# Four engines' loops written out, SyncE's kept, in a four-layer graph network

## The chip, the cores and the metric

The kernel runs on one core of one Trainium2 chip. A core has five engines, each with its own stream of instructions: TensorE (PE, matrix products; PEld is its weight load), VectorE (DVE), ScalarE (ACT), GpSimd (POOL) and SyncE (SP), which here only starts DMA transfers. They meet through semaphores. The metric is the device time of one execution in microseconds (us).

## The reference, cut to what matters

128 graphs of 64 nodes with 512 features pass four layers, each followed by a residual sum and a layer norm. Two graphs make a tile of 128 rows, so there are 64 tiles.

```python
x = _layernorm(x + _L0_gnn_ref(x, adj, W1, b1, gamma, beta, W2, b2))   # hypergraph convolution, ReLU, norm, convolution
x = _layernorm(x + _L1_gnn_ref(x, adj, w, a))                          # A = exp(leaky(8 tanh((s_i + s_j) / 8))) * adj; A @ x @ w
x = _layernorm(x + _L2_gnn_ref(x, adj, W1, b1, W2, b2, W3, b3))        # three layers adj @ (x @ W) + b
x = _layernorm(x + _L3_gnn_ref(x, nodemask, adj, adj, Wqkv, Wout, b))  # attention with 8 heads, plus adj and exp(-adj)
```

## The kernel before

Two stages stand one behind the other, with a barrier between them. `hypergraph_and_pairwise` computes layers 0 and 1 and writes its result to `x2` in HBM; `convolutions_and_attention` reads it and computes layers 2 and 3. Each stage works through 16 groups of CH = 4 tiles. Products with weights are made of three matmuls (high by high, high by low, low by high part), by `products` (L561 in the first stage, L1109 in the second); products with the 64 by 64 adjacency blocks are short ones (L581, L1140, L1171, L1185).

The order of the work is written out by hand, in a string `ORDER` in each stage. An entry such as `t2.3` is a step and a tile; a plus sign means that the tile belongs to the next group, so one pass through the string finishes a group and begins the next. Every engine goes through the same string and does its own part of each step, in `steps(entries, it, reg)`. The steps with a plus sign alone make up START, which runs first; then comes a loop of 15 turns over the whole string; then END, the steps without the sign. START and END are called with `number`, so their waits are on constants. In the loop `it` is a register, and `counts` and the lines after it (L650, L1125 on TensorE, L1016 on VectorE and so on) turn it into a few registers at the head of each turn, which the waits then use.

TensorE's first step in the loop of the first stage is `y2.2` (L561), behind `t3.0` at the end of the turn. In the second stage the string begins with `ta.0 ta.1 av.0 s.2 s.3 av.1 wo.0` and ends with `s.0+ s.1+ sm.0+ sm.1+ qk.1+`: on TensorE `ta` is L1178, `av` L1185, `s` L1171, and `qk`, `wo`, `v` and the `g` steps are L1109. In `av` TensorE waits for the copies of `ta` by ScalarE (L971) and VectorE (L1076). The loops' own instructions carry the lines L673 and L1195 on TensorE. In the first stage the run `t3.3 t2.0 t2.1` on TensorE is made of short matmuls alone (L621, L581). SyncE has loops of its own, with register values in its waits and in the addresses of its transfers.

Of the kernel before, what the change touches and what calls it, by code (L numbers as in the profile page):

```python
# [44 lines left out]
def hypergraph_and_pairwise(nc, semaphores, x, adj, W1T, b1, gamma, beta, W2T, b2, w, wT, a, x2, slots, later):  # L45
# [3 lines left out]
    iters = tiles // CH  # L49
# [5 lines left out]
    with ExitStack() as ctx:  # L55
# [161 lines left out]
        @block.gpsimd  # L217
        def _(pool):

            pool.memset(ident[:, :], 0.0).then_inc(ident0, 1)  # L220
            pool.wait_ge(ident0, 1)
            pool.affine_select(out=ident[:, :], in_=ident[:, :], compare_op=ALU.not_equal, fill=1.0, base=0,
                               pattern=[[-1, P]], channel_multiplier=1).then_inc(consts_ok, 1)
            pool.memset(ones[:, :], 1.0).then_inc(consts_ok, 1)
            pool.memset(mhalf[:, :], -0.5).then_inc(consts_ok, 1)
            pool.wait_ge(vec_in, 5 * 16)
            pool.tensor_scalar(b2_all[:, :], b2_all[:, :], 0.5, None, ALU.mult).then_inc(b2_half, 1)

            def alone(sem, value):

                pool.wait_ge(consts_ok, 3)
                pool.wait_ge(sem, value)

            def rstd(c, n, mv, ve, eps):

                alone(mv, n[c])
                pool.tensor_scalar(col(c, VE), col(c, MV + 1), eps, None, ALU.add).then_inc(ve, 1)
                pool.wait_ge(ve, n[c])
                return pool.tensor_tensor(col(c, RS), col(c, VE), mhalf[:, :], ALU.pow)

            def cur(c, n, each):

                alone(h_ok, each)
                pool.wait_ge(S_sb, each)
                pool.wait_ge(z2, n[c])
                pool.tensor_copy(CU[:, c, :], NX[:, c, :]).then_inc(cur_ok, 1)

            def u(c, n):

                pool.wait_ge(tx_ps, n[c])  # L250
                pool.wait_ge(bias_ok, n[c])
                pool.tensor_tensor(X[:, c, :], X[:, c, :], ubias[:, c, :], ALU.add).then_inc(u_ok, 1)

            def rs_first(c, n):
                rstd(c, n, mv1, ve1, EPS).then_inc(rs1, 1)

            def rs_second(c, n):
                rstd(c, n, mv2, ve2, EPS / 4).then_inc(rs2, 1)

            def rs_third(c, n):  # L260
                rstd(c, n, mv3, ve3, EPS).then_inc(rs3, 1)

            def steps(entries, it, reg):
                at, each = counts(it, reg), [reg(it + (a + 1)) for a in (0, 1)]
                for step, c, ahead in entries:
                    n = at[ahead]
                    if step == "cur":
                        cur(c, n, each[ahead])
                    if step == "u":
                        u(c, n)  # L270
                    if step == "rs1":
                        rs_first(c, n)
                    if step == "rs2":
                        rs_second(c, n)
                    if step == "rs3":
                        rs_third(c, n)

            steps(START, -1, number)
            with pool.Fori(0, iters - 1) as it:
                steps(ORDER, it, pool.to_reg)  # L280
            steps(END, iters - 1, number)

        @block.scalar
        def _(act):
# [58 lines left out]
            def steps(entries, it, reg):  # L343
                at, each = counts(it, reg), [reg(it + (a + 1)) for a in (0, 1)]
                for step, c, ahead in entries:
                    n = at[ahead]
                    if step == "w":
                        w(c)
                    if step == "S":
                        evacuate_S(each[ahead], None if entries is START else at[ahead - 1][CH - 1])  # L350
                    if step == "txe":
                        txe(c, n)
                    if step == "relu":
                        relu(c, n)
                    if step == "gs":
                        gs(c, n)
                    if step == "t2e":
                        t2e(c, n)
                    if step == "f":
                        f(c, n)  # L360
                    if step == "t3e":
                        t3e(c, n)

            steps(START, -1, number)
            with act.Fori(0, iters - 1) as it:
                steps(ORDER, it, act.to_reg)
            steps(END, iters - 1, number)

        @block.vector
        def _(dve):  # L370
# [171 lines left out]

            dve.sem_inc(z2, CH)
            steps(START, -1, number)
            with dve.Fori(0, iters - 1) as it:
                steps(ORDER, it, dve.to_reg)
            steps(END, iters - 1, number)

        @block.tensor
        def _(pe):  # L550
# [119 lines left out]
                        y3(c, n)  # L670

            steps(START, -1, number)
            with pe.Fori(0, iters - 1) as it:  # L673
                steps(ORDER, it, pe.to_reg)
            steps(END, iters - 1, number)

# [8 lines left out]
def convolutions_and_attention(nc, semaphores, x2, adj, mask_rows, mask_cols, E, AA, QK, slots, b1, b2, b3, Wqkv, bout, out):  # L686
# [4 lines left out]
    iters = tiles // CH  # L691
# [4 lines left out]
    with ExitStack() as ctx:  # L696
# [150 lines left out]
        @block.gpsimd  # L847
        def _(pool):
            pool.memset(ident[:, :], 0.0).then_inc(ident0, 1)
            pool.wait_ge(ident0, 1)  # L850
            pool.affine_select(out=ident[:, :], in_=ident[:, :], compare_op=ALU.not_equal, fill=1.0, base=0,
                               pattern=[[-1, P]], channel_multiplier=1).then_inc(consts_ok, 1)
            pool.memset(mhalf[:, :], -0.5).then_inc(consts_ok, 1)
            pool.memset(ln_ld[:, :], LN_LD).then_inc(consts_ok, 1)

            def alone(sem, value):

                pool.wait_ge(consts_ok, 3)
                pool.wait_ge(sem, value)

            def rstd(c, n, ve):

                alone(ve, n[c])
                return pool.tensor_tensor(col(c, RS), col(c, VE), mhalf[:, :], ALU.pow)  # L864

            def cm(n, loaded):

                alone(masks_in, loaded)
                pool.tensor_copy(mcf[:, :, :], mcol[:, :, :]).then_inc(mc_ok, 1)
                alone(mc_ok, n)  # L870
                pool.wait_ge(row_ok, n)
                pool.tensor_tensor(MM[:, :, :, :], MM[:, :, :, :], mcf[:, :, :].rearrange("p g c -> p c g").unsqueeze(3).to_broadcast([P, CH, 2, C]), ALU.mult)\
                    .then_inc(mm_ok, 1)
                pool.tensor_scalar(BT[:, :, :, :], A[:, :, :, :], LG, None, ALU.mult).then_inc(bt3, 1)
                alone(mm_ok, n)
                alone(exp_adj, n)
                pool.tensor_scalar(BS[:, :, :, :], MM[:, :, :, :], MASKED, -MASKED, ALU.mult, ALU.add).then_inc(bs_ok, 1)
                pool.wait_ge(bt3, n)
                pool.tensor_tensor(Cm[:, :, :, :], Cm[:, :, :, :], BT[:, :, :, :], ALU.add).then_inc(cm2, 1)
                pool.wait_ge(cm2, n)  # L880
                pool.tensor_tensor(Cm[:, :, :, :], Cm[:, :, :, :], MM[:, :, :, :], ALU.mult).then_inc(cm_ok, 1)

            def steps(entries, it, reg):
                at = counts(it, reg)
                each = [reg(it + (a + 1)) for a in (0, 1)]
                loaded = [reg(it * (16 * MASK_LOADS) + 16 * MASK_LOADS * (a + 1)) for a in (0, 1)]
                for step, c, ahead in entries:
                    n = at[ahead]
                    if step == "cm":
                        cm(each[ahead], loaded[ahead])  # L890
                    if step == "rs3":
                        rstd(c, n, ve3).then_inc(rs3, 1)
                    if step == "rs4":
                        rstd(c, n, ve4).then_inc(rs4, 1)

            steps(START, -1, number)
            with pool.Fori(0, iters - 1) as it:
                steps(ORDER, it, pool.to_reg)
            steps(END, iters - 1, number)

        def T(W, c):
# [30 lines left out]
        def _(act):  # L932
# [46 lines left out]
                act.wait_ge(load_in[k], 16)  # L979
                act.copy(qkv_parts[k][0], by_head[k]).then_inc(split_hi, 1)  # L980
            steps(START, -1, number)
            with act.Fori(0, iters - 1) as it:
                steps(ORDER, it, act.to_reg)
            steps(END, iters - 1, number)

        @block.vector
        def _(dve):
# [102 lines left out]
                            .then_inc(x4_ok, 1)  # L1090

            steps(START, -1, number)
            with dve.Fori(0, iters - 1) as it:
                steps(ORDER, it, dve.to_reg)
            steps(END, iters - 1, number)

        @block.tensor
        def _(pe):
# [93 lines left out]

            pe.wait_ge(split_lo, len(pieces) + KD)
            steps(START, -1, number)
            with pe.Fori(0, iters - 1) as it:  # L1195
                steps(ORDER, it, pe.to_reg)
            steps(END, iters - 1, number)

# [43 lines left out]
```

## Time and profile before

| | us |
|---|---|
| median of 3 runs | 2844.67 (2843.2 to 2847.39) |
| profiled execution | 2846.66 |
| its span, first to last instruction | 2844.9 |

Busy in that span: TensorE 2659.1 us, its weight loads 2197.8, VectorE 1820.5, ScalarE 879.0, GpSimd 474.9. The mean granted clock of TensorE is 0.978 of full speed. The first stage reaches to about 1150 us, the second fills the rest.

How to read the rows further down: times are us from the start of the span unless marked ns. "L1109" is line 1109 of the kernel. In a list of waits a row names the instruction that waited, what it waited for, the sum, the number of times and the longest. "issue" stands for time in which the engine waited for nothing that the profile shows. In a timeline a row has start, duration, engine, line, operation and count, and in brackets the idle time before it and its cause. The engine's sequencer, which handles branches, registers and waits, is marked by a q behind the engine's name.

### The profile page before, as it was taken

To read this page: it belongs to the slowest core of one execution; us is meant where nothing else is said; L and a number is where in the kernel's file an instruction comes from. 1 tells how busy PE (TensorE), PEld (TensorE's weight loads), DVE (VectorE), ACT (ScalarE), POOL (GpSimd) and SP (SyncE) were. 2 spreads that over 40 slices of the span, in tenths; PEclk is the share of its full clock that TensorE was granted. 3 is DMA by queue.
4 is the path that set the end of the run, shared out by engine and by line. 5 is a ranking of instruction groups with operands and counts; after the bars stand their busy time and mean duration, and the time that the engine had idled before them with its cause. 6 is when DMAs were issued, how large, how long until landed. Compare 5 with 4: busy or idle time off the path is not lost.

```text
span 2844.9 us, 73879 instructions
## 1 busy us (share of the span) xinstructions
PE 2659.1 (93%) x30296; PEld 2197.8 (77%) x30296; DVE 1820.5 (64%) x3754; ACT 879.0 (31%) x2397; POOL 474.9 (17%) x749
## 2 busy tenths in 40 slices
PE   3999999999999999299999999999999999999998
PEld 2778778777777778287788788788788778878877
DVE  3778887788878887446545655654654655565565
ACT  2222322222222222233332332333333333233233
POOL 0222222222222222010110111011011011101101
PEclk9999999999999999699999999999999999999999
DMA  5111111111111110201101100100110110110010
GB/s 181 28 38 36 35 35 35 38 36 36 38 36 40 42 35 19 97 6 33 37 8 33 38 13 28 36 25 19 33 31 13 33 38 10 29 38 17 26 32 16
DMA packets 130004, 99.41 MB, mean 35 GB/s; under 512 B 89104, under 2 KB 91152, under 8 KB 129808
## 3 DMA queue, kind: packets, MB, share of 16 engines
q1 hardware_dynamic: 129808, 96.30, 11.4%
q8 instruction: 184, 3.01, 0.5%
q14 instruction: 12, 0.10, 0.0%
HBM read 62.68 MB, written 33.55 MB: 34 GB/s over the span
## 4 chain that ended last, share of the span: by engine, by line
PE 52%; DVE 4%; issue 2%; ACT 1%; SPq 1%; DMA 0%; DVEq 0%; POOLq 0%
PE qs L1109 43%; PE qs L1140 4%; PE qs L1171 1%; PE qs L1178 1%; DVE T2l L1004 1%; PE qs L1150 1%; PE qs L1185 1%; ACT T2h L942 1%; DVE sm L1007 0%; DVE Z L1084 0%; DVE E L1069 0%; DVE E L1073 0%; DMA QK<-in_L_Wqkv 0%; DVE sm L1060 0%; DVE E L1058 0%
## 5 line engine op out<-in xcount | busy, mean ns | idle before, releaser
L1109 PE MATMUL qs<-hi,T2h 128*128 128x512 f32 x1024 | 422.0, 412 | 24.5 <-DVE T2l L1004 24.1
L1109 PE MATMUL qs<-hi,T2l 128*128 128x512 f32 x1024 | 406.9, 397 | 0.0
L1109 PE MATMUL qs<-lo,T2h 128*128 128x512 f32 x1024 | 406.5, 397 | 0.0
L1004 DVE TENSOR_TENSOR T2l<-qs,T2h 128x512 fp32r<-128x512 f32 x320 | 212.9, 687 | 183.1 <-ACT T2h L942 110.9
L864 POOL TENSOR_TENSOR sm<-sm,mhalf 128x1 f32<-128x1 f32 x128 | 86.2, 673 | 1370.6 <-DVE sm L1011 1370.6
L1109 PE MATMUL qs<-T2h,WQh 128*128 128x256 f32 x1024 | 291.2, 284 | 0.0
L1109 PE MATMUL qs<-T2h,WQl 128*128 128x256 f32 x1024 | 288.2, 281 | 0.0
L1109 PE MATMUL qs<-T2l,WQh 128*128 128x256 f32 x1024 | 288.1, 281 | 0.0
L1109 PEld LDWEIGHTS qs<-hi,T2h 128*128 128x128 f32 x1024 | 194.6, 190 | 78.5 <-DVE T2l L1004 34.8
L1109 PEld LDWEIGHTS qs<-hi,T2l 128*128 128x128 f32 x1024 | 194.5, 190 | 46.1
L1109 PEld LDWEIGHTS qs<-lo,T2h 128*128 128x128 f32 x1024 | 195.1, 190 | 39.8
L561 PE MATMUL ps<-W2h,Th 128*128 128x512 f32 x512 | 204.3, 399 | 5.1 <-issue 4.5
L561 PE MATMUL ps<-W1h,Th 128*128 128x512 f32 x512 | 206.8, 404 | 0.6 <-DVE Tl L411 0.6
L561 PE MATMUL ps<-W1l,Th 128*128 128x512 f32 x512 | 201.4, 393 | 0.0
L561 PE MATMUL ps<-W1h,Tl 128*128 128x512 f32 x512 | 201.2, 393 | 0.0
L561 PE MATMUL ps<-W2h,Tl 128*128 128x512 f32 x512 | 199.7, 390 | 0.0
L561 PE MATMUL ps<-W2l,Th 128*128 128x512 f32 x512 | 199.5, 390 | 0.0
L946 ACT ACTIVATE H<-H 128x512 f32<-128x512 f32 x128 | 81.2, 634 | 368.5 <-DVE H L1032 368.5
L1109 PEld LDWEIGHTS qs<-T2h,WQh 128*128 128x128 f32 x1024 | 192.7, 188 | 1.1
L1109 PEld LDWEIGHTS qs<-T2l,WQh 128*128 128x128 f32 x1024 | 192.8, 188 | 0.0
L1109 PEld LDWEIGHTS qs<-T2h,WQl 128*128 128x128 f32 x1024 | 192.7, 188 | 0.0
L966 ACT ACTIVATE E<-E,sm 128x64 f32<-128x64 f32 x512 | 172.0, 340 | 32.1 <-DVE sm L1062 31.6
(175 smaller groups left out, 5319.3 us busy)
## 6 DMA issues: line engine op xcount, KB each, us to landing
X<-in_x SPq DMA_DIRECT2D x64, 256.0 KB, 6.5
x<-R SPq DMA_DIRECT2D x64, 256.0 KB, 2.0
X<-x SPq DMA_DIRECT2D x64, 256.0 KB, 2.9
out<-Z SPq DMA_DIRECT2D x64, 256.0 KB, 3.1
AB<-in_adj SPq DMA_DIRECT2D x512, 8.0 KB, 1.6
A<-in_adj SPq DMA_DIRECT2D x128, 32.0 KB, 2.2
An<-in_adj SPq DMA_DIRECT2D x16, 128.0 KB, 2.3
WB<-in_adj SPq DMA_DIRECT2D x32, 64.0 KB, 7.3
```

The source lines that it names most:

```text
L561: mm = pe.matmul(out, lhsT, rhs, start=start and i == 0, stop=i == len(terms) - 1)
L864: return pool.tensor_tensor(col(c, RS), col(c, VE), mhalf[:, :], ALU.pow)
L942: act.copy(by_graph(Th, c), halves(c)).then_inc(th[i], 1)
L946: act.activation(H[:, c, :], H[:, c, :], ACT.Relu).then_inc(g_sb[i], 1)
L966: last = act.activation(EH(c)[:, h, :], EH(c)[:, h, :], ACT.Exp, bias=col(c, NB + h), scale=SCALE, accum_out=col(c, SUM + h))
L1004: return dve.tensor_tensor(lo, ps, hi.bitcast(F32), ALU.subtract)
L1109: mm = pe.matmul(out, lhsT, rhs, start=i == 0, stop=i == len(terms) - 1)
L1140: mm = pe.matmul(half[q, k * C:(k + 1) * C], rows[g, k * P + q.start:k * P + q.stop], AT[g, c, :], start=True, stop=True)
L1150: mm = pe.transpose(psA[c][:, k * P:(k + 1) * P], X[:, c, k * P:(k + 1) * P], ident[:, :])
L1171: mm = pe.matmul(ps[c][y * C:(y + 1) * C, x, (n_ * 2 + g) * C:(n_ * 2 + g + 1) * C], QK[x * C:(x + 1) * C, m, rows_g], QK[x * C:(x + 1) * ...
L1178: mm = pe.transpose(ps[c][:, x, n_ * P:(n_ + 1) * P], E[:, c, x * 2 + n_, :], ident[:, :])
L1185: mm = pe.matmul(ps[c][x * C:(x + 1) * C, g, (2 * n_ + y) * C:(2 * n_ + y + 1) * C], H[rows_g, c, h * DHEAD:(h + 1) * DHEAD], AA[rows_g, c ...
```

## The change

In both stages the loop of 15 turns is replaced by 15 calls of `steps` in a row, with plain numbers for `it`, on TensorE, VectorE, ScalarE and GpSimd. Their register instructions and branches are gone, their waits are on constants, and the order of the steps is the same. SyncE keeps its two loops. The edit is the same in eight places:

```diff
             steps(START, -1, number)
-            with pool.Fori(0, iters - 1) as it:
-                steps(ORDER, it, pool.to_reg)
+            for it in range(iters - 1):
+                steps(ORDER, it, number)
             steps(END, iters - 1, number)
...
-            with act.Fori(0, iters - 1) as it:
-                steps(ORDER, it, act.to_reg)
+            for it in range(iters - 1):
+                steps(ORDER, it, number)
...
-            with dve.Fori(0, iters - 1) as it:
-                steps(ORDER, it, dve.to_reg)
+            for it in range(iters - 1):
+                steps(ORDER, it, number)
...
-            with pe.Fori(0, iters - 1) as it:
-                steps(ORDER, it, pe.to_reg)
+            for it in range(iters - 1):
+                steps(ORDER, it, number)
```

## Rows read from the trace of the kernel before

**Rows 1.** The page's busy times: busy us, share of the span, instructions.
```profile
PE 2659.1 (93%) x30296; PEld 2197.8 (77%) x30296; DVE 1820.5 (64%) x3754; ACT 879.0 (31%) x2397; POOL 474.9 (17%) x749
```

**Rows 2.** Waits of TensorE over the whole span: total us, times, longest.
```profile
PE qs L1178 <- issue: 30.1, 14, 2.4
...
PE ps L561 <- issue: 4.5, 14, 0.4
```

**Rows 3.** The loops' own lines on TensorE (L1195, L673): ns min/median/max, first and last start.
```profile
L1195 PEldq COMPARE_BRANCH  x15: 79/3619/3799, 1375.5 to 2809.3; - x15
...
L673 PEldq COMPARE_BRANCH  x15: 76/208/245, 169.7 to 1116.3; - x15
```

**Rows 4.** The chain that ended last, second loop: start, us, what.
```profile
1267.14 11.61 PE qs L1109 x96
...
1292.48 5.86 PE qs L1109 x24
...
1366.09 11.59 PE qs L1109 x96
...
1396.51 5.86 PE qs L1109 x24
...
2799.86 11.59 PE qs L1109 x96
```

**Rows 5.** Timeline of TensorE, opening of turn 0 of the second loop.
```profile
1278.57 1.04 PE L1178 MATMUL qs<-ident,E 128*128 128x128 f32 x8
1280.08 0.69 PE L1185 MATMUL qs<-AA,H 64*64 64x64 f32 x32 [0.47 <-DVE AA L1076]
...
1281.73 0.68 PE L1185 MATMUL qs<-AA,H 64*64 64x64 f32 x32
```

**Rows 6.** Timeline of TensorE, opening of turn 2 of the second loop.
```profile
1483.69 1.09 PE L1178 MATMUL qs<-ident,E 128*128 128x128 f32 x8 [1.98 <-issue]
...
1486.56 0.27 PE L1185 MATMUL qs<-AA,H 64*64 64x64 f32 x1 [0.93 <-issue]
...
1488.24 0.68 PE L1185 MATMUL qs<-AA,H 64*64 64x64 f32 x32
```

**Rows 7.** Stretches: us, busy (count) of PE, PEld, DVE, ACT, POOL, granted clock, DMA.
```profile
187.40:255.00 67.60, 66.99 (x799) 53.94 (x791) 54.23 (x121) 19.22 (x42) 17.75 (x32) 1.00 0.12 37
1278.60:1377.60 99.00, 96.01 (x1106) 81.29 (x1104) 57.46 (x113) 34.04 (x106) 11.76 (x14) 1.00 0.10 28
...
1378.00:1396.00 18.00, 13.90 (x228) 11.28 (x228) 10.36 (x23) 5.83 (x23) 0.59 (x1) 0.81 0.06 17
```

**Rows 8.** Timeline of TensorE, `av.0` in END of the second stage.
```profile
2812.66 0.69 PE L1185 MATMUL qs<-AA,H 64*64 64x64 f32 x32 [0.33 <-ACT AA L971]
```

**Rows 9.** DMA queues in 200:1100, 118:187, 1278.6:1377.6 and 1481.7:1583.9: packets, MB, share.
```profile
q1 hardware_dynamic: 45840, 32.92, 11.7%
...
q8 instruction: 4, 0.07, 0.4%
...
q8 instruction: 10, 0.16, 0.7%
q14 instruction: 2, 0.02, 0.1%
...
q8 instruction: 11, 0.18, 0.8%
```

**Rows 10.** Timeline of TensorE, first loop: start of `S`, end of the short run.
```profile
118.69 0.28 PE L574 MATMUL ps<-HB,HT 64*64 64x64 f32 x4
...
147.57 0.45 PE L581 MATMUL ps<-CU,R 64*64 64x64 f32 x12 [0.66 <-issue]
...
187.37 0.34 PE L574 MATMUL ps<-HB,HT 64*64 64x64 f32 x6
...
213.28 2.39 PE L581 MATMUL ps<-CU,R 64*64 64x64 f32 x126
...
1066.32 0.39 PE L574 MATMUL ps<-HB,HT 64*64 64x64 f32 x7
```

More of the change, by code:

```diff
@@ L896, in _ @@
             steps(START, -1, number)
-            with pool.Fori(0, iters - 1) as it:
-                steps(ORDER, it, pool.to_reg)
+            for it in range(iters - 1):
+                steps(ORDER, it, number)
             steps(END, iters - 1, number)
@@ L981, in _ @@
             steps(START, -1, number)
-            with act.Fori(0, iters - 1) as it:
-                steps(ORDER, it, act.to_reg)
+            for it in range(iters - 1):
+                steps(ORDER, it, number)
             steps(END, iters - 1, number)
@@ L1092, in _ @@
             steps(START, -1, number)
-            with dve.Fori(0, iters - 1) as it:
-                steps(ORDER, it, dve.to_reg)
+            for it in range(iters - 1):
+                steps(ORDER, it, number)
             steps(END, iters - 1, number)
@@ L1194, in _ @@
             steps(START, -1, number)
-            with pe.Fori(0, iters - 1) as it:
-                steps(ORDER, it, pe.to_reg)
+            for it in range(iters - 1):
+                steps(ORDER, it, number)
             steps(END, iters - 1, number)
```

## Prediction, made before the changed kernel was run

> **What bounds the kernel now.** I read four views, in this order. The page's busy times: TensorE is busy 93% of the span [rows 1], so time can only go where TensorE stands still or is fed slowly, and an instruction saved on another engine counts only if TensorE waits for it. Next the waits of TensorE: of the idle time in the loops the largest item isn't a wait for data. It is 30.1 us in 14 pieces ahead of L1178, with "issue" as what ended it, and a second one of 4.5 us in 14 pieces ahead of L561 [rows 2]. A loop of 15 turns jumps back 14 times, L1178 (`ta.0`) is TensorE's first step in the second loop and L561 (`y2.2`) its first in the first loop, so these are the 28 jumps. Then the branch instructions themselves: TensorE's COMPARE_BRANCH lasts 3619 ns (median) in the second loop and 208 ns in the first [rows 3]. The last reading is the length of whole turns, because a jump may cost more than the idle time it is named for.
>
> Call the turns 0 to 14; turn 0 is entered by falling through from START, with no jump, and runs the same 1,104 matmuls on TensorE as every other (1,106 in a stretch that takes in two of its neighbours') [rows 7]. That makes it a specimen of the written-out code inside the old kernel. The last long group of `qk.1` ends at 1267.14 + 11.61 = 1278.75, the next at 1366.09 + 11.59 = 1377.68, the last at 2799.86 + 11.59 = 2811.45 [rows 4]. So turn 0 takes 98.93 us, and turns 1 to 14 take 1433.77 us, 102.41 each: a jump costs 3.48 us, not the 2.15 of the wait's name. The rows show where the rest is. In turn 0 the opening (`ta.0 ta.1 av.0 s.2 s.3 av.1`) is over at 1281.73 + 0.68 = 1282.41, 3.66 us after the turn's start [rows 5]. In turn 2 the first matmul starts after 1.98 us idle, the last matmul of `av.0` waits another 0.93 us with nothing to wait for but its own issue, and the opening ends at 1488.92, 7.2 us after the turn's start at 1481.71 [rows 6]. From the first long group of `g0.0` on, the turns are alike: 1292.48 to 1377.68 is 85.20 us in turn 0, 1396.51 to 1481.71 is 85.20 us in turn 1 [rows 4, 6]. In some turns the granted clock falls after the idle time (0.81 in the 18 us behind the first jump, against 1.00 over all of turn 0 [rows 7]); that is in the 102.41 already and goes with the idle time.
>
> Why the two loops differ is seen in the instruction packets. In the first loop, from 200 to 1100 us, there are none at all: its body stays on the chip. In the second loop a turn brings 11 packets of 16 KB on queue 8, though the code is the same each time, and turn 0 took 10 [rows 9]. Its body doesn't stay, and the jump's target has to be fetched.
>
> **The change, part by part.** *The 14 jumps of the second loop go*, and with them six register instructions at each turn's head. Price: 14 x 3.48 = 48.7 us, all on the path, since TensorE stands still or is starved there. What is late next is known from turn 0: after `ta.1` it is VectorE's copy of `ta` (0.47 us), then the chain through `z4` and `sm.2`, as now.
>
> *The register heads on VectorE.* In turn 0 `av.0` waited 0.47 us for the copy at L1076; in END, which has constants and no head, it waited 0.33 us [rows 5, 8]. The difference of 0.14 us is the nearest row: between 0 and 15 x 0.14 = 2.1 us, taken 1.5. ScalarE's and GpSimd's heads lie in their own idle time: free. Waits on constants instead of registers: the same instructions in the same number, free. SyncE keeps its loops and issues the same DMAs.
>
> *The 14 jumps of the first loop go*: the idle time before L561 is 4.5 us [rows 2], and its turns are otherwise alike, so 4.5.
>
> *What is added is a stream of instructions in the first loop*, where nothing is fetched now. TensorE has some 790 matmuls and as many weight loads a turn [rows 7], about 1,600 instructions. Turn 0 again is the specimen, since its code was fetched (4 packets [rows 9]). It takes 187.37 - 118.69 = 68.68 us, against (1066.32 - 187.37) / 13 = 67.61 for the later ones, and the difference sits in one place: in the run `t3.3 t2.0 t2.1`, 164 short matmuls with no long one between, TensorE stops for 0.66 us by "issue", and the run ends 1.03 us later in its turn (148.02 - 118.69 = 29.33, against 215.67 - 187.37 = 28.30) [rows 10]. So a fetch isn't ahead where a packet's worth of instructions goes by in about 3 us, and only this run is long enough (328 instructions, half of them weight loads). From the packets of the second loop (some 2,250 instructions with the waits, in 9 to 11 packets) a packet holds 205 to 250. It hurts when one packet's instructions lie wholly within the run: (328 - 240) / 240, somewhat over a third of the turns, since the place moves from turn to turn. I take 5 turns of 15 at 1.03; one is paid already, so +4. Bounds: -1 (never) and +14.4 (in every turn).
>
> *The same in the second loop.* Its opening is a run of some 290 instructions (16 + 64 + 128 + 64 and the waits), in which turn 0 met no stop; the other places consist mostly of long matmuls and hide a fetch, as the 10 packets of turn 0 show, behind which the turn is as long as any other. In the opening a stop would be about as dear as in the first loop: bounds 0 and 5 us, taken 1. The other engines have some 40 to 120 busy instructions a turn [rows 7], and waits beside them; turn 0 had two packets of 8 KB on queue 14 [rows 9] and the 85.20 us behind the opening are the same with and without them: free.
>
> **The sum.** -48.7 - 1.5 - 4.5 + 4 + 1 = -49.7 us. The profiled execution took 2846.66 us (span 2844.9 and 1.8 around it); it becomes 2797.0. It lies 2.0 above the median of the runs, 2844.67, so the forecast is 2795.0. With every unknown at its good end: -48.7 - 2.1 - 4.5 - 1 = -56.3, 2788. With every one at its bad end: -48.7 - 4.5 + 14.4 + 5 = -33.8, 2811.
>
> **The rivals.** *Only the named idle time goes* (30.1 + 4.5 = 34.6, result 2810): the slow opening of each turn stays, because its dense code is fetched too late whether a jump stands ahead of it or not. For it speaks that the 0.93 us stop in turn 2 is inside straight code. Against it: turn 0 has the same code fetched in a row and no such stop. 8%.
>
> *Every turn of the first loop pays the 1.03 us*: -48.7 - 1.5 - 4.5 + 14.4 + 1 = -39.3, result 2805. For it: the one specimen paid. Against: the turn's length in instructions is no multiple of a packet's, so the place moves. 8%.
>
> *Slower: the small engines are not fetched ahead.* VectorE has 121 and 113 busy instructions in a turn of the two loops and ScalarE 42 and 106 [rows 7], 382 together; at 100 to 125 in 8 KB (half the count above) that is about 50 places in 15 turns of each loop where a new packet must be there, none of them now. If each cost the 3.6 us of a fetch that nothing anticipates [rows 3], and TensorE waited for all of it, it would be +180, result 2975. It decides from 1.0 us a place. Against it: turn 0 of the second loop has two such packets and no longer tail. 4%.
>
> *The change does nothing on the path* (2845): the 3.6 us of the branch are not its own but a wait put down to it, and come up again at the head of the next turn. Against it, turn 0 once more. 3%.
>
> **How the numbers follow.** The forecast has 77%. The range reaches from the good ends, 2788, to the bad ends, 2811, and so takes in the first two rivals; what is left out is slower, no change, and something more. About 0.2% (6 us) is what a measurement of this kernel can tell from no change. Faster 0.93, same 0.03, slower 0.04.
>
> **What would show it.** No COMPARE_BRANCH on TensorE, no idle time by issue ahead of L1178; periods of 98.8 us in the second loop and 67.3 in the first, with 68.3 in about a third of its turns; stops by issue only at L581, and if in the second loop then at L1185 and L1171; queue 8 up from 184 packets to some 250, with 6 to 8 a turn in the first loop. Wrong would be: VectorE or ScalarE standing still by issue, or periods in the second loop that stay near 102.

## The result, and the profile after

The changed kernel takes 2793.89 us (median of 4 runs, 2793.61 to 2797.75) against 2844.13 for the kernel before: ratio 0.9824, interval 0.9807 to 0.9842, so 50.2 us less. The forecast was 2795.0.

The page of the changed kernel, its busy times, granted clock by 40ths of the span and instruction queues:

```profile
span 2791.6 us, 73091 instructions
...
PE 2634.4 (94%) x30296; PEld 2179.6 (78%) x30296; DVE 1814.2 (65%) x3754; ACT 875.6 (31%) x2397; POOL 474.4 (17%) x749
...
q8 instruction: 240, 3.93, 0.6%
q14 instruction: 70, 0.57, 0.1%
```

The same work in 53.3 us less of span, with 788 instructions fewer (registers and branches). Packets of instructions went from 184 to 240 on queue 8 and from 12 to 70 on queue 14. TensorE's waits (total us, times, longest), to be laid beside [rows 2]:

```profile
PE qs L1109 <- DVE T2l L1004: 29.7, 50, 1.4
PE qs L1178 <- DVE E L1073: 10.1, 17, 0.8
...
PE qs L1185 <- ACT AA L971: 5.3, 16, 0.3
...
PE qs L1140 <- issue: 3.0, 15, 0.2
...
PE ps L581 <- issue: 2.3, 2, 1.2
```

The 30.1 us ahead of L1178 and the 4.5 us ahead of L561 are gone. What is left of idle time by issue is two stops at L581 and the 3.0 us at L1140, which the kernel before has too. Where the time went is read by stretches. The timeline of TensorE after, start of turns 0 and 1 and of END in the second stage (`ta.0`):

```profile
1278.85 0.82 PE L1178 MATMUL qs<-ident,E 128*128 128x128 f32 x6
...
1377.64 0.60 PE L1178 MATMUL qs<-ident,E 128*128 128x128 f32 x4
...
2761.37 0.60 PE L1178 MATMUL qs<-ident,E 128*128 128x128 f32 x4
```

| stretch, us | before | after | difference | forecast |
|---|---|---|---|---|
| start to the second loop's first `ta.0` | 1278.6 | 1278.9 | +0.3 | -0.5 |
| the second loop's 15 turns | 1532.7 | 1482.5 | -50.2 | -49.2 |
| END of the second stage | 33.6 | 30.2 | -3.4 | 0 |
| span | 2844.9 | 2791.6 | -53.3 | -49.7 |

The turns of the second stage now last 98.8 us each (1377.64 - 1278.85 = 98.79; turns 1 to 14 (2761.37 - 1377.64) / 14 = 98.84). The first stage gained nothing. The third line isn't shown to be the change's. Stretches in END (us, busy and count of PE, PEld, DVE, ACT, POOL, granted clock, DMA), first before, then after, then a later kernel with the same second stage (e9 below):

```profile
2811.50:2844.90 33.40, 22.30 (x256) 16.75 (x254) 19.83 (x43) 9.30 (x40) 2.25 (x4) 0.80 0.09 32
```
```profile
2761.50:2791.60 30.10, 18.21 (x257) 13.63 (x255) 19.75 (x43) 9.25 (x40) 2.24 (x4) 0.99 0.10 36
```
```profile
2758.20:2791.40 33.20, 22.09 (x256) 16.85 (x254) 19.84 (x43) 9.26 (x40) 2.24 (x4) 0.80 0.08 32
```

From its first `ta.0`, END lasts 30.2 us in this execution (clock 0.99) and 33.6 in the one before (0.80). e9 has the changed code there and takes 33.4 us at 0.80; e4, whose TensorE runs the code of the kernel before, takes 30.8 at 0.91. So END varies with the clock that an execution is granted, by about as much as the single runs lie apart (2793.6 to 2797.8). This is probably also why the profiled executions differ by 53.1 us and the medians by 50.2; the unprofiled runs don't show their END.

### The profile page after: what moved, and what is told of

The parts are those of the page before. It is cut to its first block, busy times and chain, and to the rows that moved or that the text cites. A ratio compares the mean times of both kernels' runs of the same rounds, so it can differ in the third digit from the quotient of the medians.

```text
span 2791.6 us, 73091 instructions
## 1 busy us (share of the span) xinstructions
PE 2634.4 (94%) x30296; PEld 2179.6 (78%) x30296; DVE 1814.2 (65%) x3754; ACT 875.6 (31%) x2397; POOL 474.4 (17%) x749
## 4 chain that ended last, share of the span: by engine, by line
PE 50%; DVE 5%; ACT 1%; issue 1%; SPq 1%; DMA 0%; DVEq 0%; POOLq 0%; POOL 0%
PE qs L1109 43%; PE qs L1140 4%; DVE T2l L1004 1%; PE qs L1178 1%; PE qs L1150 1%; PE qs L1171 1%; DVE sm L1060 1%; DVE E L1058 1%; ACT T2h L942 1%; PE qs L1185 0%; DVE sm L1007 0%; DVE E L1069 0%; DVE E L1073 0%; DVE Z L1084 0%; DMA QK<-in_L_Wqkv 0%
## 5 line engine op out<-in xcount | busy, mean ns | idle before, releaser
L561 PE MATMUL ps<-W1h,Th 128*128 128x512 f32 x512 | 206.6, 404 | 0.6 <-DVE Tl L411 0.6
L561 PE MATMUL ps<-W2h,Th 128*128 128x512 f32 x512 | 204.5, 399 | 0.6 <-DVE Tl L441 0.6
L561 PE MATMUL ps<-W1l,Th 128*128 128x512 f32 x512 | 201.3, 393 | 0.0
L561 PE MATMUL ps<-W1h,Tl 128*128 128x512 f32 x512 | 201.2, 393 | 0.0
L561 PE MATMUL ps<-W2l,Th 128*128 128x512 f32 x512 | 199.6, 390 | 0.0
L561 PE MATMUL ps<-W2h,Tl 128*128 128x512 f32 x512 | 199.5, 390 | 0.0
```

The lines of the kernel that those rows point to most:

```text
L561: mm = pe.matmul(out, lhsT, rhs, start=start and i == 0, stop=i == len(terms) - 1)
```

## The experiments

**Each stage alone.** In e1 only the second stage is written out, in e2 only the first. The edit is that of the diff above, four places instead of eight.

> Written out on the four engines in the second stage alone; the first stage keeps its loops. My theory (what the change gained is the fetch behind TensorE's jump, which only the second stage pays, and the first stage gained nothing): within 1 us of the changed kernel, 2793 to 2795, ratio to the kernel before 0.982 to 0.983. Rival (each stage gives back its own idle time by issue, 4.5 us of it in the first): 2798.

> Written out on the four engines in the first stage alone. My theory: no change, 2844 to 2845, since what the jumps gave is taken by a chain through VectorE (f.1 sets the start of t3.1) and by two stops for instructions of 1.2 us. The rival of the first run: 4.5 us gained less 1.3 for the stops, 2841.

e2 took 2846.7 us, ratio 1.0007 (0.9997 to 1.0017): the first stage's part of the change is worth nothing, or costs a little. e1 took 2799.9 us, 0.9838 (0.9822 to 0.9854), which is 5 us over the upper end of my figure and near the rival's 2798, but not for the rival's reason. Its first loop is as before; its second loop has stops that the changed kernel doesn't have. TensorE's waits in e1, the timeline in its turn 3 (starts at 1572.2), and a row of its END (starts at 2764.9):

```profile
PE qs L1185 <- issue: 6.0, 4, 1.8
```
```profile
1573.59 0.69 PE L1185 MATMUL qs<-AA,H 64*64 64x64 f32 x32 [0.34 <-ACT AA L971]
1574.17 1.32 PE L1171 MATMUL qs<-QK 64*64 64x64 f32 x64
1575.29 0.67 PE L1185 MATMUL qs<-AA,H 64*64 64x64 f32 x30
1577.70 0.32 PE L1185 MATMUL qs<-AA,H 64*64 64x64 f32 x2 [1.75 <-issue]
...
2770.11 0.33 PE L1185 MATMUL qs<-AA,H 64*64 64x64 f32 x2 [1.48 <-issue]
```

The last two matmuls of `av.1`, at the end of the dense opening, wait 1.75 us for nothing but their issue. It happens in turns 3, 7 and 11 and once more in END, which would be turn 15: every fourth time. The 15 turns take 1489.2 us instead of 1482.5. Of these 6.7 us the three stops are 4.5; the rest follows them (turn 7 is 3.4 us longer than its neighbours with a stop of 1.75, and the granted clock is 0.91 from 1970 to 1988 us, against 1.00 at turn 3).

**TensorE alone, and all but TensorE.**

```diff
# e3: on TensorE alone, in both stages
-            with pe.Fori(0, iters - 1) as it:
-                steps(ORDER, it, pe.to_reg)
+            for it in range(iters - 1):
+                steps(ORDER, it, number)
# e4: the same on GpSimd, ScalarE and VectorE, in both stages, and not on TensorE
```

> Written out on TensorE alone, in both stages; VectorE, ScalarE and GpSimd keep loops and register waits. My theory: nearly the whole gain is TensorE's, 14 x 3.5 = 49 us less, 0 in the first stage, 2796 to 2797; the missing 2 to 3 us against the changed kernel are VectorE's register heads (0.14 a turn in each stage). Also the 0.25 us by which gs came late in turns 3, 7 and 11 of the first loop should be gone, if that was VectorE or GpSimd waiting for its own instructions. Rival (register waits and heads on all engines cost the time): much less than half of the gain, over 2820.

> The complement: written out on VectorE, ScalarE and GpSimd, TensorE keeps both loops. My theory: 0 to 2 us less, 2842 to 2844, because these engines' heads lie beside TensorE's own jump; COMPARE_BRANCH on TensorE stays at 3.6 us in the second stage. Rival (register waits and heads on all engines): over 20 us less.

e3 took 2799.4 us, 0.9843 (0.9827 to 0.986); e4 2843.9, 0.9997 (0.9987 to 1.0006). So TensorE carries the change, and the other three engines alone give nothing; COMPARE_BRANCH on TensorE stays at 3658 ns in e4. But e3 is 2 to 3 us slower than I said. Its turns of the second loop last 99.2 us instead of 98.8, and the row says whom they wait for (TensorE's waits in e3):

```profile
PE qs L1185 <- DVE AA L1076: 11.8, 17, 0.7
```

Once TensorE doesn't stop at the jump, VectorE's own head and branch come out behind it: 0.4 us a turn, 5.4 us in 15 turns. (e3 keeps ScalarE's and GpSimd's loops too; it is the row that names VectorE.) They cost nothing while TensorE's jump covers them (e4). And TensorE's waits for ScalarE's step `gs` (L306) in turns 3, 7 and 11 of the first loop, which the changed kernel and e4 show, are gone in e3. The timeline of VectorE after, in turn 3 and in turn 4 of the first loop, shows whose they were:

```profile
345.65 0.75 DVE L434 TENSOR_SCALAR R<-R,sm 128x1024 f32<-128x1024 f32 x1 [0.46 <-DVE sm L432]
```
```profile
412.65 0.21 DVE L432 BATCH_NORM_AGGREGATE sm<-sm 128x2 f32<-128x12 f32 x1
412.97 0.76 DVE L434 TENSOR_SCALAR R<-R,sm 128x1024 f32<-128x1024 f32 x1
```

In turn 3 VectorE pauses 0.46 us where it pauses 0.11 in turn 4, with the same instructions; the rest of the turn is 0.22 us late. e3 takes the pause away by keeping VectorE in its loop. In the trace of the changed kernel VectorE has 160 instructions in a turn of this loop, and the three pauses, at 345.65, 615.79 and 887.34 us, stand 640 instructions apart, which is five times 128, half of TensorE's 256 further down. So they too follow a place in the code.

**Is the jump dear because the body is large?** e5 makes TensorE's first body twice as large; e6 and e8 make its second body smaller by leaving products out (e6 the low by high product, e8 both products with a low part, everywhere in the second stage).

```diff
-            with pe.Fori(0, iters - 1) as it:
-                steps(ORDER, it, pe.to_reg)
+            with pe.Fori(0, (iters - 2) // 2) as two_turns:
+                for half in range(2):
+                    steps(ORDER, two_turns * 2 + half, pe.to_reg)
+            steps(ORDER, iters - 2, number)
```
```diff
-                return [(lh, rh), (lh, rl), (ll, rh)]
+                return [(lh, rh), (lh, rl)]        # e6;  e8: return [(lh, rh)]
```

> The kernel before, with TensorE's first loop alone made of 7 passes of two turns and the 15th turn written out behind it: half as many jumps, a body of twice the size (about 3,200 instructions against 1,600). Theory of size (a jump is dear when the body is too large to stay on the chip; 2,250 instructions are too many, 1,600 are not): COMPARE_BRANCH at L673 rises from 208 ns to about 3600, instruction packets appear in every turn of the first loop, and six jumps cost about 3 us each, so slower by 15 to 22 us, 2859 to 2866. Rival (the second stage's jump is dear for another reason, such as what stands ahead of it or the number of its registers): COMPARE_BRANCH stays near 0.2 us and the time falls by 0 to 2 us, with fewer jumps.

> The kernel before with two products in place of three in the second stage (the product of the low part of the left side with the high part of the right is left out everywhere there): TensorE's body falls from about 2,250 instructions to 1,960, with all loops as they were. Theory of size, with a limit between 1,960 and 2,250: COMPARE_BRANCH at L1195 falls from 3619 ns to about 200, no instruction packets in the second loop after its first turn, and the opening of a turn is as fast as turn 0's. The work left out is 80 x 0.23 + 64 x 0.117 = 26 us a turn, 414 in all, so 2844 - 414 - 48 = 2382. If the limit is below 1,960, or size isn't the cause: 3.6 us as before, and 2430.

> The kernel before with one product in place of three in the second stage (high by high alone), all loops as they were: TensorE's second body falls to about 1,670 instructions, near the first loop's 1,600; with 1,960 the branch was as dear as with 2,250. Theory of size (a limit between 1,600 and 1,960): COMPARE_BRANCH at L1195 about 200 ns, no packets on queue 8 in the second loop after its first turn, no idle time by issue ahead of L1178 above 0.5 us. Rival (the jump of the second stage is dear at any size): about 3.6 us as before and 28 to 30 us ahead of L1178.

e5 took 2877.1 us, 31.9 more, with half the jumps (ratio 1.0112, 1.0093 to 1.0131). The loop's own line (ns min/median/max), TensorE's waits and the instruction packets between two jumps (518.9 to 661.7 us) in e5:

```profile
L673 PEldq COMPARE_BRANCH  x7: 76/4662/5177, 234.2 to 1090.4; - x7
```
```profile
PE ps L561 <- issue: 28.2, 6, 5.5
```
```profile
q8 instruction: 15, 0.25, 0.7%
```

The same work with the same waits in the first stage, 208 ns a jump at some 1,600 instructions and 4662 at 3,200: there the size of the body is the cause. The price is higher than the second stage's (4.7 us idle a jump, not 2.15). Probably this is because the jump stands behind short matmuls that TensorE has done in 0.7 us, where the second stage's stands behind long ones; no run varied that.

e6 and e8 went the rival's way. In e6 COMPARE_BRANCH is 3554 ns and the time 2553.1 us; in e8 it is

```profile
L1195 PEldq COMPARE_BRANCH  x15: 79/3685/3890, 1322.5 to 2411.2; - x15
```
```profile
q8 instruction: 9, 0.15, 0.8%
```

with 9 packets from one jump to the next (1478.6 to 1555.3 us), so the whole body of some 1,670 instructions is brought again in each turn. The other half of the rival's forecast didn't come: no idle time by issue is left ahead of L1178 in e8, since TensorE waits there for VectorE, 135.1 us in all. e6's time is 123 us over the rival's sum. TensorE's busy time fell by 385 us, near the 414 of the sum, and its waits for others grew, among them VectorE's ahead of L1178 from 12.6 to 36.5 us. For e8, which ran once (2452.8 us), I had given no sum.

So size in instructions alone would need a limit between 1,600 and 1,670. The next experiments give a place where a packet's code seems to begin, and by that place the bodies can be counted in packets, as is done at the end of this section.

**Is it the place in the packets that makes a stop?** e9, e10 and e11 only put fulfilled waits ahead of TensorE's work, which move all later instructions. e7 is the changed kernel with TensorE's first loop kept, and e9 is e7 moved.

```diff
+            for _ in range(24):              # e9, second stage; e10: 57 and 199; e11: 14 and 242
+                pe.wait_ge(consts_ok, 3)
             pe.wait_ge(split_lo, len(pieces) + KD)
```

> The changed kernel, but TensorE keeps its loop in the first stage (208 ns a jump, nothing fetched). It gives up the jumps' 0.3 us, which VectorE's chain covers in part, and saves the two stops of 1.15 us. My theory: 2792 to 2794, 0 to 1.5 us below the changed kernel in the same call. Rival (the jump's 0.3 us counts in full): 2796 to 2797.

> The changed kernel once more, to compare the mixed one with on the same chip: 2793 to 2795.

> The mixed kernel (TensorE loops in the first stage) with 24 waits that are long fulfilled put ahead of TensorE's work in the second stage, in its 40 us of idle time there: they only move all later instructions by 24 places. Theory of place (a stop comes where a packet of 256 instructions falls wholly within the dense opening of a turn; the mixed kernel is 23 places from the changed one in the second stage, its body is 2,240 = 9 x 256 - 64 instructions, so every fourth turn is hit): the stops of turns 3, 7 and 11 go, all periods are 98.8, and the time falls by 5 to 7 us, to 2791 to 2794. Rival (those stops come from queue 1's transfers or from the loop kept in the first stage): unchanged, 2797 to 2799.

> The changed kernel with 57 fulfilled waits ahead of TensorE's first stage and 199 ahead of its second. A written-out turn of the first stage is 1,593 = 6 x 256 + 57 instructions. Theory of place: the two stops of the first stage in turns 0 and 9 (9 x 57 = 513, one more than two packets) become one, in turn 8; the second stage is shifted by 256 and shows no stop. Rival (the stops belong to what happens in these turns, such as transfers): turns 0 and 9 again.

> The changed kernel with 14 fulfilled waits ahead of TensorE's first stage and 242 ahead of its second (256 together, so the second stage stays as it is). Theory of place: the 15 turns of the first stage start at distances from a packet's edge that lie in pairs 28 apart; 14 puts none within 13 of the place that was hit. No stop by issue at L581, 2.3 us less than the changed kernel: ratio to the kernel before 0.981 to 0.982, 2790 to 2793. If the place that is hit is wider than 26, one or two stops remain, at turns 0 and 9 or 4 and 13.

e7 took 2798.2 us (0.9831, 0.9817 to 0.9844) where the changed kernel took 2793.3 beside it (0.9822, 0.9808 to 0.9835). The intervals overlap, but the trace shows e1's stops, 5.1 us in turns 3, 7 and 11 and 1.3 in END. e9 took 2790.6 (0.9813, 0.9799 to 0.9826), its 15 turns last 1482.3 us instead of 1489.1, and no stop by issue at L1185 is left. Nothing but the place of the instructions differs between the two, and the 24 waits stand in idle time.

For e10 and e11 my count of the shift was wrong. Sequencer instructions at the added line of e10, in its first and second stage:

```profile
L553 PEldq EVENT_SEMAPHORE  x27: 51/51/51, 1.6 to 4.4; - x27
...
L1196 PEldq EVENT_SEMAPHORE  x98: 51/51/51, 1158.3 to 1168.9; - x98
```

Two waits were merged into one instruction. Counted in the traces, 57 waits moved the first stage by 28 and 14 waits by 7 (and e9's 24 its second stage by 12); the second stage of e10 and of e11 was moved by 128, not by 256, and has no stop at `av`. The stops of e10 in the first stage:

```profile
416.38 0.38 PE L583 MATMUL ps<-CU,R 64*64 64x64 f32 x9 [0.87 <-issue]
...
1024.72 0.39 PE L583 MATMUL ps<-CU,R 64*64 64x64 f32 x10 [0.37 <-issue]
```

They are in turns 4 and 13; turns 0 and 9, which stop in the changed kernel, run through. I had said turn 8. With the shift of 28 the rule of place gives the right ones: a written-out turn is 6 x 256 + 57 instructions, so turns 0 and 9 are at 0 and 1 in the changed kernel, and turns 4 and 13 are at 4 x 57 + 28 = 256 and 13 x 57 + 28 = 3 x 256 + 1 in e10. In e11, at 7, turns 0, 9 (at 7 and 8), 4 and 13 (at 21 and 20 below an edge) all stop, for 0.69, 0.97, 0.60 and 0.34 us; so the place that is hit reaches from 21 below to 8 above, but not to 28 either way. Turns 4 and 13 stop one matmul behind the dense run, at the first products:

```profile
420.07 0.39 PE L563 MATMUL ps<-Wl,Th 128*128 128x512 f32 x1 [0.60 <-issue]
...
1029.56 0.50 PE L563 MATMUL ps<-Wl,Th 128*128 128x512 f32 x1 [0.34 <-issue]
```

The rival of e10, that the stops belong to their turns, is refuted. That the shifts were 28 and 7 I worked out after the runs. e10 took 2791.5 us in its one run and e11 2793.0 (0.982, 0.9807 to 0.9833).

A count of TensorE's instructions in the traces (matmuls, weight loads and the sequencer's, a loop's body counted once) says it more sharply. The stops within or right behind the dense runs come at numbers 2242 and 16577 in the changed kernel, 8642 and 22977 in e10, 2241, 8641, 16578 and 22978 in e11, and 11970, 20930, 29890 and 38850 in the second stage of e7. Each of these is a multiple of 256 plus 193 or 194. The stops in the openings of the second loop before fit as well (5058 and 5059, 194 and 195 beyond a multiple). In e5, whose turns differ in the trace by up to 26 instructions, they spread more (179 to 200).

Take these places as the edges of packets. TensorE's first body (1,599 instructions) then touches 7 packets, e8's second (some 1,670) 8, e6's (some 1,960) 9, the second body before (some 2,248) 10, and e5's first 13 or 14. From one jump to the next, 0 packets come for the first of these and 9, 10, 11 and 14 or 15 for the others: one more than the body touches. e5 has the second body of the kernel before, only moved, so that it touches 9 (it begins 4 places behind an edge), and a turn brings 10 packets instead of the 11 of [rows 9] (1519.3 to 1621.2 us in e5):

```profile
q8 instruction: 10, 0.16, 0.7%
```

So e8's body isn't only 70 instructions longer than the first one, it touches one packet more. A limit of seven packets fits all the runs and doesn't need the second stage to be different. No run moves one body from 7 to 8 packets, so that the limit goes by packets and not by instructions or by the stage isn't shown.

## Why the prediction was right, point by point

*The second loop's jumps, -48.7 and -1.5.* Right in kind and size: the 15 turns are 50.2 us shorter, and turn 0 of the kernel before was a true specimen (98.93 against 98.79 to 98.84 now, about the 0.14 of the two waits). The 0.33 us of [rows 8] is a wait for ScalarE's copy, not VectorE's, so the 0.14 is by how much VectorE's copy came behind ScalarE's, and only the least that its head can have cost. The split was wrong. I gave VectorE's head 0.1 a turn from a comparison with turn 0, which has the head but no branch. Alone, TensorE's part is worth 1532.7 - 1487.9 = 44.8 us and that of the other three engines, VectorE's by the row, the last 5.4 (e3), while their part without TensorE's is worth nothing (e4).

*The first loop's jumps, -4.5.* Wrong: they gave nothing. I asked what is late next in the second stage and not here. `y2.2` does start 0.3 us earlier, but then `t3.1` waits for VectorE's last multiplication of `f.1`. TensorE and VectorE in a turn before, and in one after:

```profile
446.57 1.16 PE L581 MATMUL ps<-CU,R 64*64 64x64 f32 x64
447.19 0.23 DVE L467 TENSOR_TENSOR Fp<-Fp,CU 128x64 f32<-128x64 f32 x1 [0.32 <-ACT Fp L320]
...
447.56 0.22 PE L621 MATMUL ps<-ones,Fp 64*64 64x1 f32 x2
```
```profile
378.83 1.16 PE L581 MATMUL ps<-CU,R 64*64 64x64 f32 x64
379.66 0.23 DVE L467 TENSOR_TENSOR Fp<-Fp,CU 128x64 f32<-128x64 f32 x1 [0.32 <-ACT Fp L320]
...
380.03 0.22 PE L621 MATMUL ps<-ones,Fp 64*64 64x1 f32 x2
```

From the run of `t2.3` to `t3.1` it is 0.99 us before and 1.20 after. After, TensorE would have gone on at 378.83 + 0.99 = 379.82, but VectorE ends at 379.89 and `t3.1` starts 0.14 behind that, so 0.21 of the 0.32 us come back.

An undisturbed turn is still shorter, 67.5 us against 67.6 [rows 10], 1.7 us in 14 turns. But that isn't the jumps'. Start of `S` in turns 1 and 3 of e3 (TensorE written out, the others in their loops) and of e4 (the reverse, with TensorE's jumps), and a wait of e3 between 187 and 1066 us:

```profile
187.06 0.22 PE L574 MATMUL ps<-HB,HT 64*64 64x64 f32 x2
...
322.37 0.23 PE L574 MATMUL ps<-HB,HT 64*64 64x64 f32 x2
```
```profile
187.93 0.27 PE L574 MATMUL ps<-HB,HT 64*64 64x64 f32 x2
...
322.91 0.28 PE L574 MATMUL ps<-HB,HT 64*64 64x64 f32 x4
```
```profile
PE ps L621 <- DVE Fp L467: 2.8, 13, 0.2
```

Two turns take 135.31 us in e3, as before (2 x 67.61 = 135.22), and 134.98 in e4, as in the changed kernel (134.96). Without its jumps TensorE only waits 0.2 us a turn more for `f.1`; the turn gets shorter where the other engines lose their register heads and branches, which I had put at nothing in this loop, and it does so with TensorE's jumps in place. e7 and e9, which keep TensorE's first loop, have the same 67.5. Idle time of an engine was again no measure of what it gives back: 2.15 was named and 3.5 came in one loop, 0.32 was named and nothing came in the other.

*The stream in the first loop, +4.* The mechanism was right (e10), the count wrong: two turns stop, not five, at 1.4 to 1.5 us each and not 1.03. I had let every packet count that lies wholly within the run, 88 places of 240; e10 and e11 give at least 30 and under 56 places of 256. Start of `S` at the ends of turn 0 and of the loop, and the stop in turn 0, after:

```profile
118.82 0.28 PE L574 MATMUL ps<-HB,HT 64*64 64x64 f32 x4
...
148.11 0.38 PE L581 MATMUL ps<-CU,R 64*64 64x64 f32 x9 [1.14 <-issue]
...
187.69 0.30 PE L574 MATMUL ps<-HB,HT 64*64 64x64 f32 x3
...
1067.13 0.34 PE L574 MATMUL ps<-HB,HT 64*64 64x64 f32 x6
```

Net of the one that was there before it is +1.8, and turns 1 to 13 last (1067.13 - 187.69) / 13 = 67.65 us, as long as before. In sum the first stage was forecast at -0.5 and came to +0.3. That the two are close is luck: of the two terms one gave nothing, the other was over twice too large, and the 1.7 us gained came from a third.

*The stream in the second loop, +1.* It was 0, by luck of the place: the same turns cost 6.6 us more in e1 and e7, somewhat over my bound of 5. Against the rival that the opening's code comes too late in straight code as well, I had said that turn 0 shows no such stop. But one turn is one place; in e1 and e7 one turn in four has it.

*The small engines, free.* Not quite, in both directions: 0.22 us lost in each of three turns of the first loop, and 0.12 gained in each, as above. The rival in which they make the kernel slower didn't occur. Those in which every turn of the first loop pays, or only the named idle time goes, didn't either. The total, 1 us beside the forecast, rests on the term of 48.7; the small ones were off by up to 4.5 us and cancelled.

## What to carry to other kernels

Look at the length of the branch instruction and at the packets of instructions in each loop before writing it out: where the body is brought again in each turn, a jump can cost more than the idle time it is named for (3.5 us here, not 2.15), and a turn that is entered without a jump (the first one) shows what the written-out code will do. Where the body stays on the chip and another engine's chain ends last, as in the first stage here, writing it out on TensorE gives nothing and adds stops. After writing out, look for stops by issue in dense runs: a few fulfilled waits in idle time ahead move them, and were worth 6.7 us here between e7 and e9, as much as an eighth of the whole change. Count the instructions between the stops: where they are multiples of one number, the place in the code is the cause.

## What the runs showed of the hardware that I had not expected

A written-out TensorE stops 0.3 to 2.0 us within runs of short matmuls, at places that recur by the count of instructions modulo 256 (turns 0 and 9, or 4 and 13, or every fourth). TensorE's second body is fetched anew in each turn at 1,670 instructions (9 packets, one more than it touches), while the first body of some 1,600 is never fetched again. VectorE, written out, pauses 0.35 us longer at three places of the first loop, 640 instructions apart. And 57 waits in a row on the same semaphore came out as some 28 instructions. The end of the kernel takes 30.2 to 33.4 us by the granted clock (0.99 to 0.80), with the same code there in the changed kernel and e9.
